# Gate data in a PSUM bank, a ramp on four banks and re-ordered queues in a gated cross-attention and LoRA-expert kernel

## The chip, the core and the metric

The kernel runs on one core of one Trainium2 chip. The metric is the device time in microseconds (us) of one execution; smaller is better.

## What is computed

x is 2x1024x2048 in float32, the context 2x2048x2048. The kernel computes, cut to what matters:

```python
def fake_quant(x, s, z): return (clip(round(x / s + z), 0, 255) - z) * s
# layer 1
q1, q2 = fake_quant(layernorm(x)), fake_quant(ctx)
x = x + tanh(g_xattn) * matmul(q1, q2)              # per batch 1024x2048 by 2048x2048
# layer 2
n = layernorm(x)
logits = n @ route_w.T                              # 8 experts
v, e = top_k(logits, 1)                             # one expert for each row
h = n @ A.T                                         # 8 experts x rank 16 = 128 columns
wh = one_hot(e) * v * h
x = x + tanh(g_ffn) * (wh @ Bw.T)
```

## The kernel before, in words

The 2048 rows of x are 16 tiles t of 128 rows; tiles 0 to 7 belong to batch 0, tiles 8 to 15 to batch 1. A *unit* (t, nb) is one tile by 512 of the 2048 output columns, 16 matmuls of 128x128 by 512, issued in four runs of four: `main(t, nb, run)`. The context of a batch comes in 16 *pieces* of 1 MB, four for each nb; each is loaded, scaled to int8 on ACT (`affine_ctx`) and widened to bf16 into `q2` on POOL or ACT (`widen_ctx`). Batch 1 overwrites the same `q2` behind the last use by tile 7.

A tile goes through these steps, and each engine has its own list of calls, written out by hand in a fixed order; an engine that waits holds everything behind it in its list:

- `load_x(t)` on the SP queue, `stats1(t)` on DVE, `first_norm(t)` on POOL, `affine_x(t)` on ACT (int8 into `x8`), `widen_x(t)` (bf16 into `q1`; DVE for tiles 0 to 3, POOL behind). Then q1 is transposed: for tiles 0 to 5 by TensorE into the two `turn` banks (`turn_q1`) and copied out by DVE (`take_q1T`), for the others by a DMA transpose on the SP queue (`flip_q1`).
- `main` on PE; `add_main(t, nb)` on DVE adds the unit to x and takes its statistics (lines 963 to 970); `stats2_sum` closes them.
- `second_norm(t)` on POOL, then for tiles 3 to 14 `norm_high` and `norm_full` on ACT, `low_rows(t)` on POOL (line 533, a 128x2048 subtraction in SBUF), and two DMA transposes `flip_high` and `flip_low`. For tiles 0, 1, 2 and 15 the transposes go through PE (`turn_y`), ACT (`high_part`) and DVE (`low_part`); for tile 15 the norm itself is done in four groups on DVE (`norm_group`).
- `h_rows_high`, `h_rows_low` (or `h_group`) on PE give h and the logits in the PSUM bank `hp`. `gate(t)` on DVE (lines 982 to 1011), a chain of 13 instructions on 128x136 or 128x128 elements and smaller, picks the expert and scales: `hl` (line 985), the maximum and its index, `pick` (993), `wh` (996), its absolute maximum, and the two halves `whs` (1007, 1009). `hl`, `pick` and `wh` are tiles in SBUF. `turn_wh` on PE (line 1459), `take_wh` on ACT, `expert_product` on PE into the two `outp` banks (1470 to 1472) and `add_experts` on DVE (1015), then `store(t)`.

PSUM has eight banks: two `mainp`, two `turn`, `hp`, `wp`, two `outp`. The unit n uses `mainp[n % 2]`, so unit n waits for the `add_main` of unit n-2. The first four tiles are worked column block by column block (`RAMP`, the *ramp*), because the context arrives only as fast as it is loaded. x tiles share eight places (`HOME`), so `load_x(t)` for t above 5 mostly waits for the store of an earlier tile. A and the router are scaled by DVE in place (`scale_a`, `scale_router`, lines 1022 and 1027).

Of the kernel before, what the change touches and what calls it, by code (L numbers as in the profile page):

```python
# [33 lines left out]
QD = 6  # L34
YD = 3
YP = {0: 0, 1: 1, 2: 2, T - 1: YD}
# [12 lines left out]

XD = 4  # L50


def build(nc, x, ctx, g_x, g_f, x1_scale, x1_zp, x2_scale, x2_zp, route_w, A, Bw, out):
# [13 lines left out]
    with st:  # L67
# [16 lines left out]
        s_half_stored = sem("half_stored")  # L84
# [54 lines left out]
        s_affine1 = sem("affine1")  # L139
        s_q1_ready = sem("q1_ready")  # L140
# [15 lines left out]
        s_y_ready = sem("y_ready")  # L156
        s_y_turned = sem("y_turned")
# [9 lines left out]
        s_h_read = sem("h_read")  # L167
# [3 lines left out]
        s_pick_done = sem("pick_done")  # L171
# [11 lines left out]
        s_outp_read = sem("outp_read")  # L183

# [20 lines left out]
        hl = sb("hl", [P, WC], f32)  # L205
# [4 lines left out]
        pick = sb("pick", [P, ER], f32)  # L210
        wh = sb("wh", [P, ER], f32)
# [4 lines left out]
        eid_i = wh[:, :].bitcast(i32)  # L216
# [7 lines left out]
        diag = pick  # L224
# [45 lines left out]
        ynq = yn[:, :, :].rearrange("p a n -> p (a n)").bitcast(bf16)  # L270
        early = [yT[:, :, :, :].rearrange("p a k m -> p (a k m)").bitcast(f32), y[:, :], stage[:, 0, :], stage[:, 1, :]]
# [34 lines left out]

        def turn_free(kind, t, b):

            if kind == "q":
                return s_q1T_dve, 2 * t + b + 1  # L310
# [4 lines left out]
            return s_y_split, 4 * YP[t] + 3 + b  # L315

# [3 lines left out]
        def _(sp):  # L320
# [35 lines left out]
            def store(t):  # L356
                sp.wait_ge(s_outp_read, NB * (t + 1))
                sp.dma_start(out_t[t], xcol(t, 0, D)).then_inc(s_stored[t % 4], 16)

            def flip_q1(t):  # L360

                sp.wait_ge(s_main_done, UNIT[t - 2, NB - 1] + 1)
# [27 lines left out]
            load_x(4)  # L390
# [3 lines left out]
            load_ctx(12)  # L394
            load_ctx(13)
# [31 lines left out]
            load_ctx(28)  # L427
            store(4)
            load_ctx(29)
            load_x(9)  # L430
            flip_high(6)
            flip_low(6)
            flip_q1(8)
            load_ctx(30)
            load_ctx(31)
            store(5)
            flip_high(7)
# [3 lines left out]
            load_x(11)  # L441
            flip_high(8)
# [3 lines left out]
            load_x(12)  # L446
            load_x(13)
            flip_high(9)
            flip_low(9)
            flip_q1(11)  # L450
            store(7)
            load_x(14)
            flip_high(10)
            flip_low(10)
            flip_q1(12)
            flip_high(11)
            store(8)
            flip_low(11)
            load_x(15)
            flip_q1(13)  # L460
# [4 lines left out]
            flip_high(13)  # L465
            flip_low(13)
# [3 lines left out]
            store(10)  # L470
# [4 lines left out]
            for half in range(2):  # L475
                sp.wait_ge(s_outp_read, NB * (T - 1) + 2 * (half + 1))
                sp.dma_start(out_t[T - 1][:, half * D // 2:(half + 1) * D // 2],
                             xcol(T - 1, half * D // 2, (half + 1) * D // 2)).then_inc(s_half_stored, 16)
            for n in range(4):
                sp.wait_ge(s_stored[n], 16 * len([t for t in range(T - 1) if t % 4 == n]))  # L480
            sp.wait_ge(s_half_stored, 32)
# [1450 lines left out]
```

## Time and profile before

| | us |
|---|---|
| median of 3 runs (389.13 to 390.45) | 389.33 |
| profiled execution, its time | 389.91 |
| profiled execution, its span | 388.10 |
| TensorE busy | 338.8 |
| VectorE busy | 292.3 |
| ScalarE busy | 186.1 |
| GpSimd busy | 166.4 |

The span is what the trace covers; the time lies 1.81 us above it. Starts are counted from the start of the span. PE is TensorE, PEld its weight loads, DVE VectorE, ACT ScalarE, POOL GpSimd, SPq the queue that issues the DMAs. L12 is line 12 of the kernel before. In a row of the timeline the square bracket gives the idle time of the engine in front of the instruction and what ended it.

### The profile page before, as it was taken

Reading aid. Unit: us, or ns where it says so; the run is one execution under the profiler, and the core shown is the slowest. Engines: PE = TensorE matmul, PEld = TensorE weight load, DVE = VectorE, ACT = ScalarE, POOL = GpSimd, SP = SyncE. Lnnn points to the kernel's source line nnn. Section 1 sums busy time; section 2 is a strip of 40 time slices with the busy share of each in tenths; the row PEclk is TensorE's granted clock in tenths of the full one; section 3 lists DMA queues with packets and bytes.
Section 4 is the critical chain, followed back from the end, with each engine's and each line's share of the span. In section 5 each row is a group of like instructions: output and inputs, shape, how many; then the busy total and the mean of one; then the engine's idle time right before and its main releaser. Section 6 shows DMA issues by size and latency. Waiting matters only on the chain.

```text
span 388.1 us, 5794 instructions
## 1 busy us (share of the span) xinstructions
PE 338.8 (87%) x2204; PEld 186.8 (48%) x2230; DVE 292.3 (75%) x578; ACT 186.1 (48%) x119; POOL 166.4 (43%) x219
## 2 busy tenths in 40 slices
PE   0169899999999879998596999999999899998883
PEld 0145344657667536435162364645464546464461
DVE  3989975787988888875688576798764566758785
ACT  1697574868668414488289442422640602440020
POOL 2766566232113740389449226183635162524000
PEclk9999999999999999999699899999999999999999
DMA  7999999096557995999989943976849961277625
GB/s 304 407 366 386 395 387 353 22 389 207 177 194 277 185 233 199 353 246 320 190 131 331 252 150 69 315 160 192 213 85 249 230 118 20 54 119 169 258 110 216
DMA packets 93618, 87.63 MB, mean 226 GB/s; under 512 B 71812, under 2 KB 72836, under 8 KB 89476
## 3 DMA queue, kind: packets, MB, share of 16 engines
q1 hardware_dynamic: 93568, 87.11, 76.4%
q8 instruction: 26, 0.43, 0.4%
q14 instruction: 12, 0.10, 0.1%
q10 hardware_dynamic: 12, 0.00, 0.0%
HBM read 52.49 MB, written 16.78 MB: 178 GB/s over the span
## 4 chain that ended last, share of the span: by engine, by line
PE 64%; DVE 19%; DMA 10%; issue 3%; ACT 2%; POOL 1%; ACTq 0%; DVEq 0%
PE main L1407 44%; DMA qa<-q 6%; PE hp L1428 3%; PE hp L1432 3%; PE hp L1429 3%; PE outp L1470 3%; PE outp L1472 2%; PE outp L1471 2%; DVE whs L1007 2%; DVE pick L993 2%; DVE bn L839 2%; DMA xs<-in_x 2%; DVE xs L1015 1%; DMA prow<-in_g_ffn 1%; DVE wh L996 1%
## 5 line engine op out<-in xcount | busy, mean ns | idle before, releaser
L1407 PE MATMUL main<-q,qa 128*128 128x512 bf16 x875 | 204.7, 387 | 6.8 <-DMA qa<-q 2.4
L1407 PEld LDWEIGHTS main<-q,qa 128*128 128x128 bf16 x896 | 87.8, 99 | 110.2 <-issue 7.2
L533 POOL TENSOR_TENSOR yn<-y,yn 128x2048 f16<-128x2048 f32 x12 | 48.9, 4075 | 32.9 <-ACT y L694 32.7
L967 DVE SCALAR_TENSOR_TENSOR xs<-main,cc,xs 128x512 f32<-128x512 f32 x52 | 38.6, 743 | 29.8 <-PE main L1407 29.6
L540 POOL CAST q<-c 128x2048 bf16<-128x2048 int8 x24 | 45.2, 1905 | 24.9 <-ACT c L650 17.1
L650 ACT ACTIVATE c<-stage,zpc,inv 128x2048 int8<-128x2048 f32 x24 | 49.6, 2086 | 11.2 <-DMA stage<-in_ctx 11.1
L518 POOL TENSOR_SCALAR ve<-mv 128x1 f32<-128x1 f32 x16 | 3.5, 220 | 90.8 <-DVE mv L974 90.8
L1015 DVE SCALAR_TENSOR_TENSOR xs<-outp,tsc,xs 128x512 f32<-128x512 f32 x52 | 36.8, 734 | 6.0 <-PE outp L1472 5.8
L688 ACT ACTIVATE yn<-xs,sc 128x2048 f16<-128x2048 f32 x10 | 20.9, 2092 | 42.5 <-POOL sc L527 42.5
L662 ACT ACTIVATE x<-xs,sc 128x2048 int8<-128x2048 f32 x13 | 27.2, 2090 | 27.6 <-POOL sc L513 25.1
L839 DVE BATCH_NORM_STATS2 bn<-xs 128x6 f32<-128x512 f32 x52 | 32.0, 676 | 7.8 <-DMA xs<-in_x 7.8
L970 DVE BATCH_NORM_STATS2 bn<-xs 128x6 f32<-128x512 f32 x52 | 36.1, 694 | 1.8
L1428 PE MATMUL hp<-WT,yT 128*128 128x136 f16 x256 | 35.8, 223 | 0.3 <-DVE yT L979 0.3
L1429 PE MATMUL hp<-WT,yT 128*128 128x136 f16 x256 | 35.8, 223 | 0.0
L699 ACT ACTIVATE whT<-wp 128x256 f16<-128x256 f16 x16 | 6.0, 378 | 61.2 <-PE wp L1459 61.2
L1470 PE MATMUL outp<-BT,whT 128*128 128x512 f16 x64 | 24.4, 380 | 5.6 <-DVE xs L1015 3.7
L550 POOL CAST q<-x 128x2048 bf16<-128x2048 int8 x12 | 22.7, 1893 | 14.9 <-ACT x L662 14.4
L1407 PE MATMUL main<-q,yn 128*128 128x512 bf16 x123 | 28.5, 379 | 0.3
L1428 PEld LDWEIGHTS hp<-WT,yT 128*128 128x128 f16 x256 | 25.0, 98 | 2.5 <-DVE yT L979 0.4
L1429 PEld LDWEIGHTS hp<-WT,yT 128*128 128x128 f16 x256 | 25.1, 98 | 2.0
L1432 PE MATMUL hp<-WT,yT 128*128 128x136 f16 x256 | 25.1, 223 | 0.0
L1471 PE MATMUL outp<-BT,whT 128*128 128x512 f16 x64 | 24.3, 379 | 0.0
(122 smaller groups left out, 423.6 us busy)
## 6 DMA issues: line engine op xcount, KB each, us to landing
stage<-in_ctx SPq DMA_DIRECT2D x24, 1024.0 KB, 7.6
xs<-in_x SPq DMA_DIRECT2D x13, 1024.0 KB, 6.7
out<-xs SPq DMA_DIRECT2D x12, 1024.0 KB, 5.7
yT<-in_ctx SPq DMA_DIRECT2D x4, 1024.0 KB, 10.6
y<-in_ctx SPq DMA_DIRECT2D x4, 1024.0 KB, 10.6
c<-in_x SPq DMA_DIRECT2D x3, 1024.0 KB, 7.1
out<-c SPq DMA_DIRECT2D x3, 1024.0 KB, 6.3
c<-in_L_ffn_A SPq DMA_DIRECT2D x1, 1024.0 KB, 15.9
```

The costliest lines, as they stand in the source:

```text
L533: pool.tensor_tensor(yn[:, 1, :], y[:, :], yn[:, 0, :], ALU.subtract).then_inc(s_ylo_made, 1)
L540: pool.tensor_copy(in_q2(piece), c8_of(piece)).then_inc(s_ctx_ready, 1)
L650: act.activation(c8_of(piece), place(piece), ACT.Identity, bias=zpc[:, 1:2], scale=inv[:, 1:2])\
L839: dve.bn_stats(bn1[:, t % 2, nb, :], xcol(t, nb * NW, (nb + 1) * NW)).then_inc(s_bn1_done, 1)
L967: dve.scalar_tensor_tensor(out=xcol(t, c0, c1), in0=mainp[n % 2][:, :], scalar=cc[:, :], in1=xcol(t, c0, c1), op0=ALU.mult, op1=ALU.add).t ...
L970: dve.bn_stats(bn2[:, t % G, nb, :], xcol(t, c0, c1)).then_inc(s_bn2_done, 1)
L1015: dve.scalar_tensor_tensor(out=xcol(t, g * NW, (g + 1) * NW), in0=outp[g % 2][:, :], scalar=tsc[:, t:t + 1], in1=xcol(t, g * NW, (g + 1) * ...
L1407: last = pe.matmul(mainp[n % 2][:, :], q1T(t)[:, k, :], q2[:, nb, k, :], start=(k == 0), stop=(k == KC - 1))
L1428: pe.matmul(hp[:, 0:WC], yT[:, 0, c, :], WT[:, c, 0:WC], start=(c == 0), stop=False)
L1429: pe.matmul(hp[:, 0:WC], yT[:, 0, c, :], WT[:, c, WC:2 * WC], start=False, stop=False)
L1432: return pe.matmul(hp[:, 0:WC], yT[:, 1, c, :], WT[:, c, 0:WC], start=False, stop=(c == KC - 1))
L1470: pe.matmul(o, whT[:, 0, :], BT[:, 0, g * NW:(g + 1) * NW], start=True, stop=False)
```

## The change

- **Gate.** `hl` and `wh` become column ranges of the PSUM bank `hp` (columns 144 to 279 and 288 to 415, behind h's 0 to 135). `pick` and its instruction go: one `scalar_tensor_tensor` writes `wh` = (index equal) * hl, and the factor top8, which pick carried, goes into `tsc`. The gate has 12 instructions. The next tile's h, which overwrites the bank, now waits for `s_wh_ready` (the gate's end) where it waited for `s_h_read` (its first instruction).
- **First tile.** `affine_x(0)` and `widen_x(0)` are split in two halves of 1024 columns, `turn_q1(t, half)` and `take_q1T(t, half)` are separate calls, and `main(t, 0, run)` waits for the half of q1T that it reads.
- **Four banks.** Units 0 to 11 rotate over `mainp` and `outp`; `spread_scales`, which uses `outp[0]`, waits for the `add_main` of unit 11.
- **ACT.** It scales A and the router (`mult_a`, `mult_router`) in place of DVE, and takes the last group of tile 15's norm.
- **Orders.** All five lists are re-ordered. The last store goes out in four parts in place of two. Among the moves on the SP queue: `load_x(4)` goes behind four more pieces, `load_ctx(25)` and `load_ctx(26)` ahead of `load_x(6)` and `load_x(7)`, `load_x(9)` behind `flip_q1(8)`, `flip_high(6)` ahead of `store(4)`, `flip_q1(13)` ahead of `load_x(15)`. On PE the two units in work are interleaved run by run in many tiles; `turn_q1(2)` goes behind the first run of `main`.

```diff
+N4 = 12
...
-        hl = sb("hl", [P, WC], f32)
...
-        pick = sb("pick", [P, ER], f32)
-        wh = sb("wh", [P, ER], f32)
...
         hp = bank("hp")
+        hl, wh = hp[:, 144:144 + WC], hp[:, 288:288 + ER]
...
+        ramp_banks = mainp + outp
...
+        def bank_of(n):
+            return ramp_banks[n % 4] if n < N4 else mainp[n % 2]
...
             def gate(t):
+
                 n = t + 1
                 dve.wait_ge(s_h_done, n)
-                dve.tensor_tensor(hl[:, :], hp[:, 0:WC], wscale[:, :], ALU.mult).then_inc(s_h_read, 1)
-                dve.wait_ge(s_h_read, n)
+                dve.tensor_tensor(hl, hp[:, 0:WC], wscale[:, :], ALU.mult).then_inc(s_hl_done, 1)
+                dve.wait_ge(s_hl_done, n)
...
-                dve.tensor_scalar(pick[:, :], eid[:, :], idxf[:, :], top8[:, 0:1], ALU.is_equal, ALU.mult)\
-                   .then_inc(s_pick_done, 1)
-                dve.wait_ge(s_pick_done, n)
-                dve.tensor_tensor(wh[:, :], hl[:, 0:ER], pick[:, :], ALU.mult).then_inc(s_wh_done, 1)
+                dve.scalar_tensor_tensor(out=wh, in0=eid[:, :], scalar=idxf[:, :], in1=hl[:, 0:ER],
+                                         op0=ALU.is_equal, op1=ALU.mult).then_inc(s_wh_done, 1)
...
-                dve.tensor_scalar(tsc[:, t:t + 1], am[:, 1:2], th[:, 1:2], None, ALU.mult).then_inc(s_tsc_done, 1)
+                dve.tensor_scalar(tsc[:, t:t + 1], am[:, 1:2], th[:, 1:2], top8[:, 0:1], ALU.mult, ALU.mult)\
+                   .then_inc(s_tsc_done, 1)
...
-                dve.tensor_scalar(whs[:, 0, :], wh[:, :], am[:, 2:3], None, ALU.mult).then_inc(s_wh_high, 1)
+                dve.tensor_scalar(whs[:, 0, :], wh, am[:, 2:3], None, ALU.mult).then_inc(s_wh_high, 1)
...
             def h_rows_high(t):
-                pe.wait_ge(s_h_read, t)
-                pe.wait_ge(s_yhiT_loaded, 16 * (t - YD + 1))
+                pe.wait_ge(s_wh_ready, t)
+                pe.wait_ge(s_yhiT_loaded, 16 * (YN.index(t) + 1))
...
+            def affine_first(half):
+                c0, c1 = half * D // 2, (half + 1) * D // 2
+                act.wait_ge(s_norm1, 1)
+                act.activation(x8[:, c0:c1], xcol(0, c0, c1), ACT.Identity, bias=sc1[:, 0, 2:3], scale=sc1[:, 0, 1:2])\
+                   .then_inc(s_affine1 if half else s_affine_half, 1)
...
+            def mult_a():
+                act.wait_ge(s_consts, 4)
+                act.wait_ge(s_wmax_step, 3)
+                act.activation(a_nat, a_nat, ACT.Identity, bias=zero[:, :], scale=wmax[:, 2:3]).then_inc(s_a_scaled, 1)
...
-            turn_q1(0)
-            turn_q1(1)
-            turn_q1(2)
+            turn_q1(0, 0)
+            turn_q1(0, 1)
+            turn_q1(1, 0)
+            turn_q1(1, 1)
             column_sums(0, [0])
             main(0, 0, 0)
+            turn_q1(2, 0)
+            turn_q1(2, 1)
             main(0, 0, 1)
-            turn_q1(3)
```

## Rows read from the trace of the kernel before

**Rows 1.** The page: busy time, share of the span and instructions.
```profile
PE 338.8 (87%) x2204; PEld 186.8 (48%) x2230; DVE 292.3 (75%) x578; ACT 186.1 (48%) x119; POOL 166.4 (43%) x219
```

**Rows 2.** Waits of PE: line, what ended them, us in total, times, longest.
```profile
PE wp L1459 <- DVE whs L1009: 11.0, 3, 5.5
...
PE outp L1470 <- DVE xs L1015: 3.7, 3, 2.3
PE main L1407 <- DMA qa<-q: 2.4, 3, 1.3
...
PE main L1407 <- DVE xs L967: 1.4, 2, 1.1
...
PE outp L1470 <- DVE c L1015: 0.9, 1, 0.9
```

**Rows 3.** Stretches: length, busy by engine (instructions), PE clock, DMA share, GB/s.
```profile
125.00:155.00 30.00, 26.57 (x201) 15.14 (x201) 25.27 (x62) 10.68 (x7) 12.86 (x13) 1.00 0.85 210
155.00:187.00 32.00, 27.33 (x161) 13.69 (x161) 23.12 (x41) 23.84 (x13) 23.48 (x28) 1.00 1.02 304
187.00:220.00 33.00, 27.02 (x142) 12.96 (x144) 24.41 (x36) 21.82 (x14) 17.85 (x17) 0.84 1.01 212
```

**Rows 4.** Gate instructions by line: duration in ns, min/median/max.
```profile
L993 DVE TENSOR_SCALAR pick<-eid,idxf,top x16: 345/346/3601, 98.4 to 377.8; 128x128 f32<-128x128 f32 x16
L996 DVE TENSOR_TENSOR wh<-hl,pick x16: 291/292/1866, 98.8 to 378.1; 128x128 f32<-128x128 f32 x16
L1007 DVE TENSOR_SCALAR whs<-wh,am x16: 285/286/4105, 99.8 to 379.2; 128x128 f16<-128x128 f32 x16
```

**Rows 5.** Timeline around tile 5's gate, POOL, then DVE (start, us).
```profile
178.96 4.08 POOL L533 TENSOR_TENSOR yn<-y,yn 128x2048 f16<-128x2048 f32 x1
182.98 5.63 POOL L540 CAST q<-c 128x2048 bf16<-128x2048 int8 x3
...
180.92 2.20 DVE L993 TENSOR_SCALAR pick<-eid,idxf,top 128x128 f32<-128x128 f32 x1
183.16 1.86 DVE L996 TENSOR_TENSOR wh<-hl,pick 128x128 f32<-128x128 f32 x1
...
186.88 1.86 DVE L1009 SCALAR_TENSOR_TENSOR whs<-wh,am,whs 128x128 f16<-128x128 f32 x1
```

**Rows 6.** Timeline of PE: both long stalls and the matmuls behind them.
```profile
188.81 0.40 PE L1459 MATMUL wp<-idh,whs 128*128 128x128 f16 x2 [5.47 <-DVE whs L1009]
189.47 9.59 PE L1407 MATMUL main<-q,qa 128*128 128x512 bf16 x32 [0.27 <-DVE xs L967]
...
214.21 0.29 PE L1459 MATMUL wp<-idh,whs 128*128 128x128 f16 x2 [3.69 <-DVE whs L1009]
...
216.61 7.34 PE L1407 MATMUL main<-q,qa 128*128 128x512 bf16 x29 [0.22 <-issue]
...
347.19 7.07 PE L1407 MATMUL main<-q,qa 128*128 128x512 bf16 x32
```

**Rows 7.** Timeline of the ramp: PE, and POOL's widening of piece 7.
```profile
24.94 1.86 PE L1337 MATMUL turn<-idb,q 128*128 128x128 bf16 x16 [3.35 <-DVE qa L884]
26.60 3.62 PE L1407 MATMUL main<-q,qa 128*128 128x512 bf16 x8
...
46.89 4.26 PE L1407 MATMUL main<-q,qa 128*128 128x512 bf16 x19
...
41.84 2.01 POOL L540 CAST q<-c 128x2048 bf16<-128x2048 int8 x1 [0.81 <-ACT c L650]
```

**Rows 8.** Timeline of the SP queue: one DMA transpose of q1.
```profile
297.36 5.55 SPq L364 DMA_TRANSPOSE qa<-q x1
```

**Rows 9.** Timeline of DVE in the tail, then the last stores.
```profile
368.86 1.00 DVE L1060 TENSOR_SCALAR y<-xs,sc 128x512 f32<-128x512 f32 x2
...
376.75 0.30 DVE L985 TENSOR_TENSOR hl<-hp,wscale 128x136 f32<-128x136 f32 x1 [0.43 <-PE hp L1432]
...
383.19 1.41 DVE L1015 SCALAR_TENSOR_TENSOR xs<-outp,tsc,xs 128x512 f32<-128x512 f32 x2 [0.26 <-PE outp L1472]
```

More of the change, by code:

```diff
@@ L441, in _ @@
             load_x(11)
+            load_x(12)
             flip_high(8)
@@ L455, in _ @@
             flip_q1(12)
+            store(7)
+            store(8)
+            load_x(14)
             flip_high(11)
-            store(8)
             flip_low(11)
+            flip_q1(13)
             load_x(15)
-            flip_q1(13)
             store(9)
@@ L783, in _ @@
             widen_ctx(18)
+            affine_ctx(28)
+            take_wh(5)
             widen_ctx(19)
@@ L827, in _ @@
             high_part(15, 0)
-            take_wh(14)
             high_part(15, 1)
+            norm_group(15, 3)
             high_part(15, 2)
             high_part(15, 3)
+            take_wh(14)
             take_wh(15)
@@ L1026, in scale_router, with mult_a, mult_router @@
                 scale_of(rmax, r_nat, s_rmax_step)
+            def mult_a():
+                dve.tensor_scalar(a_nat, a_nat, wmax[:, 2:3], None, ALU.mult).then_inc(s_a_scaled, 1)
+            def mult_router():
                 dve.tensor_scalar(r_nat, r_nat, rmax[:, 2:3], None, ALU.mult).then_inc(s_r_scaled, 1)
@@ L1139, in _ @@
             low_part(1, 3)
-            stats1(5)
+            add_main(4, 1)
+            gate(1)
             add_experts(0, 0)
-            gate(1)
             add_experts(0, 1)
@@ L1276, in _ @@
             add_main(14, 2)
-            add_experts(11, 3)
+            add_experts(11, 0)
+            add_experts(11, 1)
             add_main(14, 3)
             stats2_sum(14)
+            add_experts(11, 2)
+            gate(13)
+            tile_terms(15)
+            add_main(15, 0)
+            add_experts(11, 3)
             add_experts(12, 0)
@@ L1282, in _ @@
             add_experts(12, 2)
-            gate(13)
-            tile_terms(15)
-            add_main(15, 0)
             add_main(15, 1)
@@ L1329, in wait_turn, with turn_q1 @@
                     pe.wait_ge(s, count)
-            def turn_q1(t):
-                pe.wait_ge(s_q1_ready, t + 1)
-                for half in range(2):
-                    wait_turn("q", t, half)
-                    for k in range(KC // 2):
-                        c = half * KC // 2 + k
-                        last = pe.transpose(turnb[half][:, k * P:(k + 1) * P], q1[:, c * P:(c + 1) * P], idb[:, :])
-                    last.then_inc(s_q1T_turned, 1)
+            def turn_q1(t, half):
+                if t == 0 and half == 0:
+                    pe.wait_ge(s_q1_half, 1)
+                elif t == 0 or half == 0:
+                    pe.wait_ge(s_q1_ready, t + 1)
+                wait_turn("q", t, half)
+                for k in range(KC // 2):
+                    c = half * KC // 2 + k
+                    last = pe.transpose(turnb[half][:, k * P:(k + 1) * P], q1[:, c * P:(c + 1) * P], idb[:, :])
+                last.then_inc(s_q1T_turned, 1)
             def turn_a(c):
@@ L1556, in _ @@
             main(1, 3, 2)
+            main(1, 3, 3)
             spread_scales()
-            turn_q1(4)
-            main(1, 3, 3)
             column_sums(2, [3])
@@ L1875, in _ @@
             main(15, 1, 1)
+            main(15, 2, 0)
             main(15, 1, 2)
             main(15, 1, 3)
-            main(15, 2, 0)
+            expert_product(12, 1)
             main(15, 2, 1)
+            expert_product(12, 2)
+            expert_product(12, 3)
+            turn_wh(13)
             h_rows_high(14)
```

689 lines of the change are left out of this document (383 added, 306 removed).

## The prediction

> **What bounds the kernel now.** I read the page first: TensorE is busy 338.8 of 388.1 us, the next engine, DVE, 292.3 [rows 1]. So PE is the bound, and a change is worth what it takes from PE's 49.3 idle us or from matmul time at the low clock. The waits of PE say where the idle time behind the ramp lies: turn_wh (line 1459) waits for the end of the gate three times, 11.0 us; expert products wait for add_experts, 3.7 and 0.9 us; main waits for a DMA transpose 2.4 us and for add_main 1.4 us [rows 2]. Next the stretches: 155 to 187 and 187 to 220 hold 4.7 and 6.0 us of idle PE, and the second runs at a mean clock of 0.84 [rows 3]. Last the gate's own instructions. Three of them have a median of 0.29 to 0.35 us and a longest of 1.87 to 4.11 us [rows 4]. In tile 5's gate pick takes 2.20, wh 1.86 and the second whs 1.86 us, while POOL runs a 4.08 us subtraction in SBUF and then three casts one after the other; pick ends at 183.12, where POOL goes from the one to the other, and the next long ones end with casts [rows 5]. I read this as a shared resource: a gate instruction that needs it waits for POOL's instruction to end.
>
> The Trainium skill, page "SBUF — State Buffer", section "Who interferes with whom", has the rule: VectorE and GpSimd share one pair of SBUF ports as an exclusive lock, and a VectorE instruction takes it in a two-port mode or with two SBUF inputs. The rows fit (a tensor_scalar, a tensor_tensor and a scalar_tensor_tensor with two SBUF inputs are the long ones), and by it the new gate is free, since every instruction over 128 columns has hl or wh in PSUM as an input and at most one input in SBUF.
>
> **Gate.** It runs 16 times. pick goes (0.35 us each), and the waits for POOL go. What that is worth is read on PE. Tile 5: stall of 5.47, then 0.27 waiting for add_main, which stood behind the gate; then 32 matmuls in 9.59 us, where 32 elsewhere take 7.07: 2.5 us, at 1.2 in place of 2.4 GHz for part of it, after PE had stood still [rows 6]. Tile 6: 3.69, then 0.22; then the 36 matmuls to the next expert product last from 214.50 to 223.95, 9.45 us less the 0.22, where 36 at full clock take 36/32 x 7.07 = 7.95: 1.3 us [rows 6]. Tile 4: pick took up to 3.60 us [rows 4], and an expert product then waited 2.3 for add_experts [rows 2]. Tile 13: the first whs took 4.11 [rows 4], and main then waited 1.1 for add_main [rows 2]. Sum: 5.47 + 0.27 + 2.5 + 3.69 + 0.22 + 1.3 + 2.3 + 1.1 = **16.9 us**, all on the path. The third wait of line 1459, 11.0 - 5.47 - 3.69 = 1.8 us, is the last tile's gate and belongs to the tail.
>
> Whether an instruction that reads and writes PSUM costs more: hl, which reads PSUM, takes 0.30 us for 136 columns [rows 9], wh from SBUF 0.29 for 128 [rows 4]. I take no difference; 0.1 us an instruction would be 0.6 us a gate, hidden for all tiles but the last.
>
> The skill speaks against the change here: "VectorE: DVE Perf Modes", section "The TRN2 errata", gives a VectorE instruction with a PSUM source a fixed part of 120 cycles where an SBUF source has 58. The two rows above don't show it at this size. By the page's figures, an estimate, about 62 cycles at 0.96 GHz on five or so instructions would add 0.3 us to each gate and to the end of the kernel.
>
> The added wait: h of tile t+1 may start only when gate t is done, some 2.4 us later than before. Behind it on PE stands the whole rest of the list. In the new list turn_wh(t), which waits for the same event anyway, stands ahead of h(t+1) for most tiles; where it doesn't (h of tiles 1, 3, 13 and 15), at least 16 matmuls of main lie between, 3.5 us at 7.07 for 32 [rows 6]. Taken at nothing; rival 3 prices it where this cover is gone.
>
> **Ramp.** Before, the first main starts at 26.60 because turn_q1(2) stands ahead of it and waits 3.35 us for DVE [rows 7]. After, main(0,0,0) needs only the first half of tile 0's q1T and piece 0, both ready by then, and stands behind turn_q1(1); I put it at about 24.2. A fixed end bounds the gain: main(0,1,3), the fourth run that needs piece 7, starts at 46.89, and piece 7 is widened at 41.84 + 2.01 = 43.85; its load runs with the DMA queues full. So at most 3.0 us can come out at that point, 4.0 if the piece lands 1 us earlier (its buffer comes free before affine_x(3) now). The four banks and the two scalings moved to ACT serve to reach it: they take the add_main wait of the ramp away. At the other end is 0, if DVE, which has the same casts and copies to do, sets the pace. I take **2.5 us**, near the upper bound, because the waits of PE behind the ramp are all priced below and none of them is for a piece [rows 2]. mult_a and mult_router (an estimate of 2 us each, four times the 0.50 us of 512 columns in norm_group [rows 9]) lie in ACT's waits for pieces; without that cover they delay a piece by up to 4 us, and that too is the 0 end.
>
> **Flips and loads.** Of the 2.4 us of waits for a transposed q1 and the 0.9 for an expert product, the new SP order removes what stands behind `load_x(15)`: that transpose took 5.55 us to issue alone [rows 8], and it now goes first. The others depend on x loads, which wait for stores. I take **1.5 us**; between 0 and 3.3.
>
> **Tail.** From norm_group(15,0) at 368.86 to the last gate's start at 376.75 are 7.9 us [rows 9]. DVE has in between four groups, four expert adds and four low parts. The new order leaves it three groups, three adds (two of them behind the last low part) and four low parts: 0.5 us less for the group, 0.7 for the add; pick takes 0.35 off the last gate, and the last store is a quarter of a tile in place of a half, perhaps 0.5 us sooner down. But two expert adds of tile 14 go behind the gate, 1.4 us more on DVE after it. Terms that are independent of each other: +1.2 +0.4 +0.5, and of the two adds about half hidden under turn_wh, take_wh and the first product: -0.7. **1.4 us**, between 0 and 2.
>
> **What comes late next.** Without the stalls PE reaches main(8) about 14 us sooner after main(7) and the pieces of batch 1, x(8), x(9) and the flips must be there. The DMA queues are full for the whole of 155 to 220, share 1.02 and 1.01 [rows 3]. The new order moves two loads ahead of it and x(9) behind the flips; 125 to 155 has 0.15 x 30 = 4.5 us of free queue. New small stalls are likely: x(6) is now behind piece 25, one more megabyte, up to 2.6 us at gate(2) by my walk through the lists. I add back **3.0 us**, between 0 and 10.
>
> **The sum.** 16.9 + 2.5 + 1.5 + 1.4 - 3.0 = 19.3 us. Against the profiled execution: 389.9 - 19.3 = 370.6; the median lies 0.6 below that execution, so **370.0 us**.
>
> **Rivals.**
> 1. *The DMA queues become the bound of 155 to 220.* For it: both shares at 1.0 [rows 3], and 14 of the 16.9 us lie there. Then of these 14 only the 4.5 us of free queue before can be won, 9.5 come back in place of my 3.0: 370.0 + 6.5 = 376.5. Against it: part of the share is transposes, which nobody waited for more than 1.3 us [rows 2], and the loads stand in a better order. Chance 0.22.
> 2. *The gate still waits for POOL.* If the lock isn't a matter of SBUF inputs, wh and both whs can still be held; only pick's share goes (3.60 - 0.35 and 2.20 - 0.35 us in tiles 4 and 5 [rows 4, 5]). The stalls of tiles 5, 6 and 13 then stay for the most part, some 11 of the 16.9: 381. Against it: hl, with one input in PSUM, stands in the same gates and was never long, and neither were the adds from PSUM. 0.07.
> 3. *The bank that h and the gate share stops PE.* If h(t+1) stands right behind h(t), it waits the gate out: 2.4 us x 15 = 36 us, less the 19.3: 389.3 + 16.7 = 406. It decides from where PE comes to h(t+1) less than 2.7 us after h(t); eight tiles of it cancel the gain. Against it: a tile's 64 matmuls of main, 14 us, lie between them for most tiles. 0.04, with 0.02 for a smaller form that ends within 0.3%.
>
> **Chances and range.** Forecast 0.65 (364 to 373), rivals 0.22, 0.07 and 0.06. The measurement can tell 0.3%, 1.2 us, from no change. Faster by more 0.94, within 0.02, slower 0.04. The low end takes all upper bounds without the add-back: 389.3 - 16.9 - 4.0 - 3.3 - 2.0 = 363.1; the high end takes rival 1 with the lower bounds of the ramp: 379. Range 364 to 379.
>
> **What the profile after would show.** Gate: no instruction of it above 0.4 us, line 993's kind gone, DVE busy at most 292 less the 12 us that the five long ones of rows 4 and 5 lose, 5.5 for pick and 4 for the scalings, 271 us, no wait on turn_wh over 1 us but in the tail. Clock 1.00 between 187 and 220. Ramp: first main near 24, the run main(0,1,3) near 44. Rival 1: main waiting for flips or widened pieces between 150 and 205. Rival 2: long whs or wh with POOL busy beside them. Rival 3: h waiting for whs. Wrong would be the prediction if PE's idle time between 50 and 350 came out above 8 us.

## The result and the profile after

The changed kernel takes 371.79 us (median of 4 runs, 370.97 to 372.98). The kernel before, run beside it on the same chip, takes 389.89 (389.13 to 390.77). The ratio is 0.9537, with a 95% interval of 0.9498 to 0.9577. The profiled execution took 371.14 us with a span of 369.4, against 389.9 and 388.1 before: 18.7 us are gone from the span. The forecast was 19.3 us for the profiled execution and 370.0 for the median.

First the page of the kernel after, busy time by engine, to be laid beside [rows 1]:

```profile
PE 334.0 (90%) x2230; PEld 185.6 (50%) x2230; DVE 266.6 (72%) x560; ACT 190.9 (52%) x123; POOL 166.0 (45%) x219
```

PE has the same matmuls to do (the smaller count in [rows 1] is one of records) and spends 4.8 us less on them; the rest of the gain is idle time. DVE lost 25.7 us of busy time, of which pick (5.5) and the two scalings (4) are 9.5 by the prediction's estimate. Most of the rest is time that gate instructions had spent held up: the four kinds of lines 993, 996, 1007 and 1009, whose tiles all lay in SBUF, took 38.8 us before, 18.4 more than 16 times their medians. The forecast was at most 271 us of busy DVE; it is 266.6.

The waits of PE in the kernel after (line, what ended them, us in total, times, longest), beside [rows 2]:

```profile
PE outp L1442 <- DMA prow<-in_g_ffn: 8.4, 1, 8.4
PE turn L1462 <- DVE qa L990: 6.1, 1, 6.1
PE turn L1462 <- DVE q L981: 5.7, 1, 5.7
PE turn L1554 <- DVE y L1177: 2.6, 1, 2.6
PE main L1534 <- DMA qa<-q: 2.0, 2, 1.3
PE outp L1601 <- DVE xs L1127: 1.8, 2, 1.6
PE main L1534 <- POOL q L584: 1.6, 2, 0.9
PE outp L1601 <- ACT whT L763: 1.0, 2, 0.5
PE main L1534 <- DVE xs L1073: 0.9, 1, 0.9
PE outp L1601 <- DVE c L1127: 0.4, 1, 0.4
```

The top line of [rows 2], 11.0 us of turn_wh waiting for the gate, has no successor here. The first three lines are the start of the kernel. Line 1554 and the 1.6 of line 1601 are the tail.

The three stretches of [rows 3], after (length, busy by engine with instructions, PE clock, DMA share, GB/s):

```profile
125.00:155.00 30.00, 29.60 (x213) 16.53 (x211) 23.58 (x61) 14.45 (x9) 10.88 (x18) 1.00 0.97 252
155.00:187.00 32.00, 29.73 (x173) 14.59 (x172) 20.45 (x41) 22.91 (x15) 23.95 (x24) 1.00 1.02 263
187.00:220.00 33.00, 32.24 (x222) 17.65 (x220) 24.14 (x55) 23.04 (x13) 19.99 (x27) 1.00 1.01 287
```

PE's idle time falls from 3.4, 4.7 and 6.0 us to 0.4, 2.3 and 0.8, and the clock of the last stretch from 0.84 of full speed is back at 1.00. The DMA share of the last two was already 1.0 and stays there. Between 50 and 350, the stretch for which the prediction had named 8 us of idle PE as the sign of being wrong, PE is idle for 6.0 us (16.4 before).

The gate's instructions over 128 columns besides hl and the reduction, by line (ns, min/median/max), the answer to [rows 4]. The data of hl and wh now lie in the tile hp:

```profile
L1106 DVE SCALAR_TENSOR_TENSOR hp<-eid,idxf,hp x16: 356/356/356, 100.4 to 356.6; 128x128 f32<-128x128 f32 x16
L1119 DVE TENSOR_SCALAR whs<-hp,am x16: 341/342/343, 101.5 to 357.8; 128x128 f16<-128x128 f32 x16
L1121 DVE SCALAR_TENSOR_TENSOR whs<-hp,am,whs x16: 350/351/352, 101.9 to 358.2; 128x128 f16<-128x128 f32 x16
```

Minimum and maximum of each line are now within 2 ns of each other, where the maxima were 1.87 to 4.11 us.

Timeline of the kernel after, PE, then POOL's widening of piece 7 (start, us; idle time before in brackets), beside [rows 6, 7]:

```profile
24.23 1.91 PE L1534 MATMUL main<-q,qa 128*128 128x512 bf16 x4
...
43.91 1.03 PE L1534 MATMUL outp<-q,qa 128*128 128x512 bf16 x4
...
158.61 3.63 PE L1534 MATMUL main<-q,qa 128*128 128x512 bf16 x16 [0.90 <-DVE xs L1073]
...
169.60 3.63 PE L1534 MATMUL main<-q,qa 128*128 128x512 bf16 x16 [1.28 <-DMA qa<-q]
...
211.69 7.08 PE L1534 MATMUL main<-q,qa 128*128 128x512 bf16 x32 [0.76 <-DMA qa<-q]
...
340.93 4.48 PE L1534 MATMUL main<-q,qa 128*128 128x512 bf16 x20
...
349.26 1.11 PE L1554 MATMUL turn<-idf,y 128*128 128x128 f32 x8 [2.55 <-DVE y L1177]
...
41.56 1.89 POOL L584 CAST q<-c 128x2048 bf16<-128x2048 int8 x1 [1.23 <-ACT c L705]
```

The rows cut the span in three parts at main(0,1,3) and at the end of the last run of main. The latter ends at 340.93 + 4.48 = 345.41 in the kernel after. In the kernel before it is this row, which ends at 365.44:

```profile
361.82 3.62 PE L1407 MATMUL main<-q,qa 128*128 128x512 bf16 x16
```

| part of the span | before, us | after, us | difference | forecast |
|---|---|---|---|---|
| start to main(0,1,3) | 46.89 | 43.91 | -3.0 | -2.5 |
| from there to the end of main | 318.55 | 301.50 | -17.0 | -16.9 - 1.5 + 3.0 = -15.4 |
| end of main to the end | 22.66 | 23.99 | **+1.3** | **-1.4** |
| span | 388.1 | 369.4 | -18.7 | -19.3 |

The tail moved against the forecast. DVE of the kernel after in its last 21 us, the answer to [rows 9], and then the SP queue of the stores (start and length of the issue):

```profile
348.65 1.00 DVE L1177 TENSOR_SCALAR y<-xs,sc 128x512 f32<-128x512 f32 x2
...
355.62 0.31 DVE L1098 TENSOR_TENSOR hp<-hp,wscale 128x136 f32<-128x136 f32 x1 [0.20 <-PE hp L1562]
...
358.44 1.40 DVE L1127 SCALAR_TENSOR_TENSOR xs<-outp,tsc,xs 128x512 f32<-128x512 f32 x2
360.10 1.41 DVE L1127 SCALAR_TENSOR_TENSOR xs<-outp,tsc,xs 128x512 f32<-128x512 f32 x2 [0.26 <-PE outp L1603]
362.17 1.41 DVE L1127 SCALAR_TENSOR_TENSOR xs<-outp,tsc,xs 128x512 f32<-128x512 f32 x2 [0.66 <-PE outp L1603]
363.83 1.41 DVE L1127 SCALAR_TENSOR_TENSOR xs<-outp,tsc,xs 128x512 f32<-128x512 f32 x2 [0.26 <-PE outp L1603]
...
355.44 6.42 SPq L402 DMA_DIRECT2D out<-xs  x2
362.94 2.79 SPq L521 DMA_DIRECT2D out<-xs  x4
```

The SP queue of the kernel before in its tail:

```profile
371.21 10.31 SPq L358 DMA_DIRECT2D out<-xs  x2
382.96 2.00 SPq L477 DMA_DIRECT2D out<-xs  x2
```

From norm_group(15,0) to the start of the last gate are now 7.0 us (7.9 before), 0.9 of the 1.2 us that the sum had. Behind the gate stand eight adds in place of six. The first SP row of each fence holds store(13) and store(14). store(14) is out at 355.44 + 6.42 = 361.86, that is 6.2 us after the gate's start; before it was 371.21 + 10.31 = 381.52, 4.8 us after 376.75. From there to the end of the span are 7.5 us, before 6.6. So the tail reads -1.1 (end of main to the gate) + 1.5 + 0.9 = +1.3.

### The profile page after: what moved, and what is told of

Read it like the earlier page. It is cut to its first block, busy times and chain, and to the rows that moved or that the text cites. A ratio compares the mean times of both kernels' runs of the same rounds, so it can differ in the third digit from the quotient of the medians.

```text
span 369.4 us, 5825 instructions
## 1 busy us (share of the span) xinstructions
PE 334.0 (90%) x2230; PEld 185.6 (50%) x2230; DVE 266.6 (72%) x560; ACT 190.9 (52%) x123; POOL 166.0 (45%) x219
## 4 chain that ended last, share of the span: by engine, by line
PE 65%; DMA 11%; POOL 9%; DVE 6%; ACT 3%; issue 2%; SPq 1%; ACTq 0%; POOLq 0%; DVEq 0%
PE main L1534 40%; PE outp L1534 6%; POOL q L584 4%; DMA xs<-in_x 4%; DMA qa<-q 3%; PE hp L1558 3%; PE hp L1559 3%; PE hp L1562 3%; DMA out<-xs 3%; PE outp L1601 2%; POOL yn L577 2%; PE outp L1603 2%; PE outp L1602 2%; DMA prow<-in_g_ffn 2%; PE turn L1554 2%
## 5 line engine op out<-in xcount | busy, mean ns | idle before, releaser
L1534 PE MATMUL main<-q,qa 128*128 128x512 bf16 x880 | 199.5, 380 | 4.6 <-DMA qa<-q 2.0
L1534 PEld LDWEIGHTS main<-q,qa 128*128 128x128 bf16 x880 | 85.0, 98 | 104.7 <-DMA qa<-q 3.0
L705 ACT ACTIVATE c<-stage,zpc,inv 128x2048 int8<-128x2048 f32 x24 | 49.8, 2087 | 11.3 <-DMA stage<-in_ctx 11.3
L584 POOL CAST q<-c 128x2048 bf16<-128x2048 int8 x24 | 46.1, 1937 | 17.7 <-ACT c L705 16.8
L1073 DVE SCALAR_TENSOR_TENSOR xs<-main,cc,xs 128x512 f32<-128x512 f32 x46 | 34.1, 741 | 21.2 <-PE main L1534 20.7
L1127 DVE SCALAR_TENSOR_TENSOR xs<-outp,tsc,xs 128x512 f32<-128x512 f32 x52 | 36.9, 739 | 14.2 <-PE outp L1603 14.1
L723 ACT ACTIVATE x<-xs,sc 128x2048 int8<-128x2048 f32 x12 | 25.0, 2087 | 17.1 <-POOL sc L557 12.1
L592 POOL CAST q<-x 128x2048 bf16<-128x2048 int8 x12 | 22.7, 1891 | 24.1 <-ACT x L723 18.0
L1601 PE MATMUL outp<-BT,whT 128*128 128x512 f16 x64 | 24.3, 380 | 3.2 <-DVE xs L1127 1.8
L1602 PE MATMUL outp<-BT,whT 128*128 128x512 f16 x64 | 24.3, 379 | 0.0
L1603 PE MATMUL outp<-BT,whT 128*128 128x512 f16 x64 | 24.3, 379 | 0.0
```

The costliest lines, as they stand in the source:

```text
L584: pool.tensor_copy(in_q2(piece), c8_of(piece)).then_inc(s_ctx_ready, 1)
L705: act.activation(c8_of(piece), place(piece), ACT.Identity, bias=zpc[:, 1:2], scale=inv[:, 1:2])\
L1073: dve.scalar_tensor_tensor(out=xcol(t, c0, c1), in0=bank_of(n)[:, :], scalar=cc[:, :], in1=xcol(t, c0, c1), op0=ALU.mult, op1=ALU.add).the ...
L1127: dve.scalar_tensor_tensor(out=xcol(t, g * NW, (g + 1) * NW), in0=outp[g % 2][:, :], scalar=tsc[:, t:t + 1], in1=xcol(t, g * NW, (g + 1) * ...
L1534: last = pe.matmul(bank_of(n)[:, :], q1T(t)[:, k, :], q2[:, nb, k, :], start=(k == 0), stop=(k == KC - 1))
L1601: pe.matmul(o, whT[:, 0, :], BT[:, 0, g * NW:(g + 1) * NW], start=True, stop=False)
```

## The experiments

The theory under test: most of the gain comes from the place of the gate's data, since a gate instruction is held up by POOL only where all its tiles lie in SBUF. Its rivals are the wait of h, the new orders of the queues, and the ramp. Ratios are to the kernel before run beside each, with 95% intervals. The experiments ran on several chips, so two versions are compared by the difference of their ratios, times 389.9; the difference of the medians stands beside it where the two disagree.

**gate_only.** The kernel before with the gate of the kernel after, and the wait that it needs. Ramp, orders and stores stay. Two helpers that had borrowed the room of wh and pick get tiles of their own, as in the kernel after.

```diff
-        hl = sb("hl", [P, WC], f32)
...
-        pick = sb("pick", [P, ER], f32)
-        wh = sb("wh", [P, ER], f32)
...
+        hl, wh = hp[:, 144:144 + WC], hp[:, 288:288 + ER]
...
-                dve.tensor_scalar(pick[:, :], eid[:, :], idxf[:, :], top8[:, 0:1], ALU.is_equal, ALU.mult)\
-                   .then_inc(s_pick_done, 1)
-                dve.wait_ge(s_pick_done, n)
-                dve.tensor_tensor(wh[:, :], hl[:, 0:ER], pick[:, :], ALU.mult).then_inc(s_wh_done, 1)
+                dve.scalar_tensor_tensor(out=wh, in0=eid[:, :], scalar=idxf[:, :], in1=hl[:, 0:ER],
+                                         op0=ALU.is_equal, op1=ALU.mult).then_inc(s_wh_done, 1)
...
-                    pe.wait_ge(s_h_read, t)
+                    pe.wait_ge(s_wh_ready, t)
```

> The kernel before with the gate of the change alone (hl and wh in the PSUM bank of h, pick folded into wh, h waiting for the gate's end); every list in its old order. Theory (the shared resource cost 16.9 us): the two long waits for whs (5.47 and 3.69 us) and the low clock between 187 and 220 go, no gate instruction lasts over 0.4 us; up to 16.9 us less, and what is late next in the old order takes 2 to 4 of it back: 373 to 377 us against 389.9. Rival (the new orders made the gain, the gate only fits into them): 383 us or more.

Measured: 376.20 us, ratio 0.9640 (0.9590 to 0.9689), span 373.7. One row of PE's timeline of this kernel, the longest wait behind the ramp:

```profile
191.04 0.22 PE L1424 MATMUL hp<-WT,yT 128*128 128x136 f16 x1 [3.09 <-DMA yT<-yn]
```

No gate instruction lasts over 0.36 us. The gate alone is worth 0.036 x 389.9 = 14.0 us (12.1 to 16.0 by the interval). The row is what then comes late: h(6) waits for its transposed tile, which stands in the old SP order behind a store and an x load. Its last main ends at 351.28, so 14.2 us are won up to there and 0.3 in the tail (22.4 us for 22.7).

**gate_pick_sbuf.** The same with hl and wh in PSUM, but pick kept as it was, a tensor_scalar from SBUF to SBUF (shown against gate_only; the factor top8 goes back from `tsc` into pick):

```diff
-                dve.scalar_tensor_tensor(out=wh, in0=eid[:, :], scalar=idxf[:, :], in1=hl[:, 0:ER],
-                                         op0=ALU.is_equal, op1=ALU.mult).then_inc(s_wh_done, 1)
+                dve.tensor_scalar(pick[:, :], eid[:, :], idxf[:, :], top8[:, 0:1], ALU.is_equal, ALU.mult)\
+                   .then_inc(s_pick_done, 1)
+                dve.wait_ge(s_pick_done, n)
+                dve.tensor_tensor(wh, hl[:, 0:ER], pick[:, :], ALU.mult).then_inc(s_wh_done, 1)
```

> As gate_only, but pick stays: an instruction with one SBUF input and an SBUF output. Theory (an instruction is held by POOL when it reads SBUF alone into SBUF, or reads two SBUF inputs): pick stays long in the gates of tiles 4 to 6 (up to 3.6 us), wh and both whs stay at 0.3 to 0.4 us; the time lies between gate_only and before, 376 to 383 us. Rival (anything that touches the bank or the timing of h is what freed the gate): no long pick, same time as gate_only plus 16 x 0.35 us of DVE at most.

Measured: 381.16 us, ratio 0.9749 (0.9710 to 0.9788). Two of its gate instructions by line, as above:

```profile
L992 DVE TENSOR_SCALAR pick<-eid,idxf,top x16: 344/347/4123, 98.1 to 367.1; 128x128 f32<-128x128 f32 x16
L1006 DVE TENSOR_SCALAR whs<-hp,am x16: 349/351/353, 99.5 to 368.6; 128x128 f16<-128x128 f32 x16
```

In one kernel two instructions of one kind: the one between SBUF tiles is held up to 4.1 us, the one that reads PSUM never. The longest pick starts at 136.40, 0.04 us behind a 4.07 us subtraction of POOL. Of PE's waits, turn_wh has 4.3 us (1.7 in gate_only) and the expert products wait 4.2 us for add_experts (1.4). Against gate_only only pick and its factor differ, and that costs 0.0109 x 389.9 = 4.2 us. So the place of the operands is the cause of the long instructions. Not every kind is held in SBUF: the reduction read `wh` there before and never took over 0.289 us, in tile 5's gate at 185.05 too, in the middle of POOL's casts [rows 5].

**wait_only.** The kernel before, with the new wait of h alone.

```diff
-                    pe.wait_ge(s_h_read, t)
+                    pe.wait_ge(s_wh_ready, t)
```

> The kernel before with one edit: h of the next tile waits for the gate's end (s_wh_ready) and not for its first instruction. Theory (taken at nothing): within 0.5 us of before, 389 to 391 us, no wait of h for whs over 0.5 us in total. Rival (the held bank costs PE): up to 2.4 us a tile, over 393 us.

Measured: 389.93 us, ratio 0.9985 (0.9960 to 1.0010), span 387.6. No wait on an h appears that was not there before. The cover holds in the old lists; the kernel after, with the new ones, shows no wait on h either, and rival 3 falls.

**after_gate_sbuf.** The kernel after, hl and wh moved back to SBUF. The fused instruction, all orders and the ramp stay.

```diff
-        hl, wh = hp[:, 144:144 + WC], hp[:, 288:288 + ER]
+        hl_t, wh_t = sb("hl", [P, WC], f32), sb("wh", [P, ER], f32)
+        hl, wh = hl_t[:, :], wh_t[:, :]
```

> The kernel after the change with hl and wh as tiles in SBUF again, all else (orders, folded pick, four banks) as changed. Theory: wh (two SBUF inputs) and both whs are held by POOL again where they overlap its subtractions and casts, single instructions of 1.8 to 4 us return, and 6 to 15 us come back: 378 to 387 us. Rival (the orders keep gates and POOL apart by themselves): 372 us, no long instruction.

Measured: 389.56 us, ratio 0.9967 (0.9939 to 0.9994), span 390.1. Its timeline around one gate (POOL, DVE, PE), and then its PE clock in two stretches:

```profile
182.12 4.07 POOL L578 TENSOR_TENSOR yn<-y,yn 128x2048 f16<-128x2048 f32 x1
182.23 4.11 DVE L1107 SCALAR_TENSOR_TENSOR wh<-eid,idxf,hl 128x128 f32<-128x128 f32 x1
186.13 5.68 POOL L585 CAST q<-c 128x2048 bf16<-128x2048 int8 x3
188.20 1.86 DVE L1122 SCALAR_TENSOR_TENSOR whs<-wh,am,whs 128x128 f16<-128x128 f32 x1
190.12 0.40 PE L1590 MATMUL wp<-idh,whs 128*128 128x128 f16 x2 [5.47 <-DVE whs L1122]
190.78 9.24 PE L1535 MATMUL main<-q,qa 128*128 128x512 bf16 x32 [0.27 <-DVE xs L1074]
```
```profile
125.00:155.00 30.00, 26.79 (x180) 14.41 (x181) 22.54 (x47) 10.79 (x7) 9.62 (x15) 0.89 0.73 179
187.00:220.00 33.00, 27.64 (x172) 14.50 (x174) 23.93 (x40) 22.46 (x13) 20.10 (x19) 0.90 0.62 180
```

The fused instruction begins 0.11 us after POOL's subtraction and ends with it (186.34 and 186.19). PE stands still for the same 5.47 us as in [rows 6], and the 32 matmuls behind it take 9.24. The answer is clear and the size was missed: nearly the whole gain is gone, (0.9967 - 0.9537) x 389.9 = 16.8 us (17.8 by the medians), where 6 to 15 were expected. In the new order other gates meet POOL (add_main is waited for 5.8 us in total, in four places, where [rows 2] has 1.4). So all the other parts of the change together are worth (0.9640 - 0.9537) x 389.9 = 4.0 us once the gate is free (4.4 by the medians), and 0.33% of 389.9, 1.3 us, while it is not. The two figures differ by less than their intervals allow for, so that these parts are worth more once the gate is free is suggested, not shown.

**two_banks.** The kernel after without the four banks of the ramp.

```diff
-N4 = 12
+N4 = 0
```

> The kernel after the change with N4 = 0: the ramp's units use two banks again. Theory: the ramp's 3.0 us need the four banks in part, because DVE falls behind with copies and scalings; PE waits for add_main again between 35 and 44, main(0,1,3) starts 0.5 to 2 us later than 43.9, and so does the end: 372.5 to 374 us. Rival (the order alone does it): within 0.3 us of the changed kernel.

Measured: 373.49 us, ratio 0.9546 (0.9503 to 0.9589), span 371.9. main(0,1,3) starts at 44.30, 0.4 us later, and add_main is waited for three times, 1.5 us, in place of once, 0.9. The median lies 1.7 above that of the kernel after, the ratio only 0.0009, 0.4 us, and the intervals overlap, so a gain of the banks beyond the 0.4 us at the ramp isn't shown.

**first_whole.** The kernel after with tile 0 scaled and widened in one piece.

```diff
-            affine_first(0)
-            affine_first(1)
+            affine_x(0)
...
-            widen_first(0)
-            widen_first(1)
+            widen_x(0)
```

> The kernel after the change with the first tile scaled and widened whole. Theory: turn_q1(0) starts 0.4 us later, but turn_q1(1) waits for DVE's copy behind stats1(3) until 22.5 in any case, and piece 7 comes at 43.9: no change of the time, within 0.3 us. Rival (the halves carry part of the ramp's gain): 0.5 to 1.3 us slower.

Measured: 371.75 us, ratio 0.9504 (0.9454 to 0.9554), span 369.7, main(0,1,3) at 43.68. The halves do nothing that shows.

**scale_dve.** The kernel after with mult_a and mult_router back on DVE.

```diff
             affine_ctx(4)
-            mult_a()
...
             scale_a()
+            mult_a()
...
             affine_ctx(10)
-            mult_router()
...
             scale_router()
+            mult_router()
```

> The kernel after the change with A and the router scaled by DVE again, directly behind their maxima. Theory: 2.3 and 1.6 us more in DVE's list at 31 and 36; four banks cover part; main(0,1,3) 0 to 2 us later, 372 to 374 us. Rival (ACT's cover was not free: pieces come sooner without it): 0.5 us faster.

Measured: 372.29 us, ratio 0.9527 (0.9483 to 0.9572), span 369.9. main(0,1,3) moves to 45.00, 1.1 us later, and the median doesn't follow; no difference is shown.

**x9_early.** The kernel after, with the SP order of before around flip_high(6).

```diff
-            flip_high(6)
             store(4)
+            load_x(9)
+            flip_high(6)
             flip_low(6)
             flip_q1(8)
-            load_x(9)
```

> The kernel after the change with three SP steps in the old order: store(4), load_x(9), and only then flip_high(6), flip_low(6), flip_q1(8). Theory (the queue order around tile 8 is what keeps the full DMA queues from becoming the bound): flip_high(6) waits for the store's landing, 6 to 8 us later than 176.1, main(8) or h(6) waits 1 to 4 us, 373 to 376 us. Rival (the queues have slack there): within 0.5 us.

Measured: 375.13 us, ratio 0.9583 (0.9529 to 0.9636), span 373.4. The SP queue in this kernel, PE behind it, and then the SP queue of the kernel after:

```profile
181.97 0.33 SPq L374 DMA_DIRECT2D xs<-in_x  x1
182.40 5.00 SPq L413 DMA_TRANSPOSE yT<-yn  x1
...
189.60 0.22 PE L1558 MATMUL hp<-WT,yT 128*128 128x136 f16 x1 [2.28 <-DMA yT<-yn]
```
```profile
176.09 1.86 SPq L413 DMA_TRANSPOSE yT<-yn  x1
178.00 1.07 SPq L402 DMA_DIRECT2D out<-xs  x1
```

The transpose goes out 6.3 us later, takes 5.00 us to issue in place of 1.86, and PE waits for it, as h(6) did in gate_only. The last main ends at 348.22, 2.8 us later. By the traces this one order carries the greater part of the 4.0 us of the other parts. By the ratios it is 0.0046, 1.8 us, by the medians 3.3, and the intervals overlap: its size stays open, though each of its four times (373.24 to 375.99) lies above each of the kernel after (370.97 to 372.98).

**old_tail.** The kernel after, with the lists of DVE, PE and ACT before and around gate(15) in the order of before (and all four LN2 groups on DVE).

```diff
-LAST_ACT = [3]
+LAST_ACT = []
...
-            gate(15)
             add_experts(14, 0)
...
             add_experts(14, 1)
+            gate(15)
             add_experts(14, 2)
             add_experts(14, 3)
```

> The kernel after the change with the lists of PE, DVE and ACT from expert_product(13,2) on as before the change (all four norm groups on DVE, two of tile 14's adds ahead of the last gate). From the end of main(15) to the end of the span the kernel before takes 22.7 us and the changed one 24.0. Theory (eight adds behind the last gate in place of six cost more than the shorter way to the gate gives): 1 to 1.7 us faster than the changed kernel. Rival (the last stores are what is late): no faster.

Measured: 370.21 us, ratio 0.9498 (0.9476 to 0.9520), span 368.0. Its SP queue:

```profile
350.44 10.12 SPq L402 DMA_DIRECT2D out<-xs  x2
361.34 3.07 SPq L521 DMA_DIRECT2D out<-xs  x4
```

Its gate starts later (355.98, 11.3 us after its last main, where the kernel after has 10.2), yet store(14) is out at 360.56, 1.3 us sooner than in the kernel after, and the tail is 23.3 us for 24.0. The median is 1.6 us lower, the ratio 0.0039, and the two intervals overlap by 0.2%: a gain is likely, by span and median alike, but not shown beyond doubt.

**halves.** The kernel after, with the last store in two parts as before.

```diff
-            for g in range(NB):
-                sp.wait_ge(s_outp_read, NB * (len(OUT_DVE) - 1) + g + 1)
...
+            for half in range(2):
+                sp.wait_ge(s_outp_read, NB * (len(OUT_DVE) - 1) + 2 * (half + 1))
...
```

> The kernel after the change with the last store in two parts. In the changed kernel the last add ends at 365.24 and the span at 369.40, 4.2 us; before it was 384.6 and 388.1, 3.5 us. Theory (the quarters queue behind store(14), which now goes out 3.5 us before the last add, and gain nothing): within 0.4 us of the changed kernel. Rival (the four parts cost issue time): 0.4 to 0.7 us faster.

Measured: 371.24 us, ratio 0.9530 (0.9506 to 0.9553), span 368.9. From the end of store(14)'s issue, 356.10 + 6.26 = 362.36, to the end are 6.5 us, where the kernel after has 7.5. But its store(14) comes 0.5 us later, behind a stretch at low clock. The same window of its trace and of the kernel after's (columns as in [rows 3]):

```profile
349.00:352.00 3.00, 3.00 (x12) 1.68 (x11) 2.19 (x4) 1.90 (x3) 0.00 (x0) 0.53 0.03 5
```
```profile
349.00:352.00 3.00, 2.74 (x18) 1.81 (x18) 2.97 (x6) 1.78 (x3) 0.00 (x0) 1.00 0.02 5
```

In both PE had stood still for 2.6 us, until 348.29 in halves and until 349.26 in the kernel after. In the one PE then runs at about 1.2 GHz and gets 12 matmuls done, in the other at 2.4 GHz and 18. In the median nothing is shown: 0.6 us, with overlapping intervals.

**act_pool_tail.** The kernel after, with the expert part of tile 14 scaled by ACT and added by POOL, so that DVE has no add of tile 14 left.

```diff
-OUT_ACT = []
+OUT_ACT = [14]
...
-            add_experts(14, 0)
-            add_experts(14, 1)
-            add_experts(14, 2)
-            add_experts(14, 3)
...
+            add_part(14, 0)
+            add_part(14, 1)
+            add_part(14, 2)
+            add_part(14, 3)
```

> The kernel after the change with tile 14's expert adds off DVE: ACT scales each product out of PSUM (0.6 us), POOL adds it to x (1.0 us by a quarter of its 4.08 us subtraction). Theory (DVE's adds behind the last gate and store(14) behind them are what is late): store(14) goes out 1 us sooner and the four adds behind the gate are tile 15's alone; 2 us faster than the changed kernel, 369 to 370 us. Rival (POOL's adds hold DVE or come late, or the last stores' bytes are the bound): no faster than 0.5 us.

Measured: 373.41 us, ratio 0.9576 (0.9549 to 0.9604), span 371.6: slower than the kernel after, if anything. Its rows of POOL and SP:

```profile
358.87 4.94 POOL L604 TENSOR_TENSOR xs<-xs,yn 128x512 f32<-128x512 f32 x4 [11.30 <-ACT yn L814]
...
356.45 7.71 SPq L402 DMA_DIRECT2D out<-xs  x2
```

One add on POOL takes 1.26 us, where DVE's takes 0.74, and store(14) is out at 364.16 in place of 361.86. The theory that any relief of DVE behind the gate helps falls in this form: the tile is waited for, not the engine. Part of the 2.2 us that its span is longer is a low clock here too (0.50 between 349 and 352); how much isn't told apart.

**old_tail_halves.** Both edits together: the old order of the tail and two parts of the last store.

```diff
-LAST_ACT = [3]
+LAST_ACT = []
...
-            gate(15)
             add_experts(14, 0)
...
             add_experts(14, 1)
+            gate(15)
...
-            for g in range(NB):
...
+            for half in range(2):
...
```

> old_tail with the last store in two parts. From the end of the issue of store(14) to the end of the span lie 7.5 us in the changed kernel, 7.4 in old_tail, 7.4 in act_pool_tail, all with four parts, and 6.5 with two parts (halves) and 6.6 before. Theory (the last two stores, 2 MB, are late as a whole, and four parts cost them 0.9 us): 0.6 to 0.9 us faster than old_tail, 369.3 to 369.6 us, span 367.1. Rival (the last add plus a fixed landing is the end): the same as old_tail.

Measured: 369.78 us (369.05 to 370.65), ratio 0.9489 (0.9460 to 0.9518), span 368.2. It is the fastest version of the study, 2.0 us or 0.5% below the median of the kernel after. Its interval overlaps that of the kernel after by 0.2%, and it can't be told from old_tail (370.21), where 0.6 to 0.9 us less were expected. In its profiled execution the last expert products of tile 15 fell on a low clock; its window, and old_tail's:

```profile
361.00:363.00 2.00, 2.00 (x6) 0.59 (x5) 1.16 (x2) 0.00 (x0) 0.00 (x0) 0.50 0.95 393
```
```profile
361.00:363.00 2.00, 1.65 (x7) 0.42 (x6) 1.74 (x4) 0.00 (x0) 0.00 (x0) 1.00 1.03 422
```

So its last add ends at 365.03, 1.4 us after old_tail's (363.64). From the end of store(14)'s issue, 360.65, to the end of the span are then 7.5 us although the last store has two parts, and 3.2 from the last add.

## Why the prediction was right, and where it was not

**What bounds the kernel** was read rightly: PE, with its idle time between 155 and 220 and the low clock behind it.

**Gate, 16.9 us.** Right in mechanism and nearly in size. gate_only won 14.0 with the old orders, and the loss of the gate's place in the new kernel cost 16.8 by the ratios; the term of 16.9 stands at the upper end. What was counted is PE's standstill plus the slow matmuls behind it, and not the time of the gate's own instructions; that was the right measure. The Trainium skill's rule on who holds the SBUF ports ("SBUF — State Buffer", "Who interferes with whom"), by which the new gate is free, is borne out by gate_pick_sbuf: the one SBUF-to-SBUF tensor_scalar reaches 4123 ns, the PSUM one 353.

**No difference for operands in PSUM.** Nearly. By the medians hl, which read PSUM before too and now also writes it, took 0.307 us (0.299 before), wh 0.356 (0.352 in SBUF in after_gate_sbuf), the reduction 0.291 (0.286), the second whs 0.351 (0.350). One did change: the first whs, a tensor_scalar, took 0.342 in place of 0.286. The Trainium skill's page "VectorE: DVE Perf Modes" ("The TRN2 errata") spoke against the change with 62 cycles more for each instruction, an estimated 0.065 us. The first whs shows 0.056 and the others 0.00 to 0.01, so the trace doesn't agree for most of them. `tsc`, which now takes a second scalar operand, went from 0.194 to 0.255.

**Added wait, nothing.** Right, shown by wait_only for the old lists and by the waits of the kernel after for the new ones.

**Ramp, 2.5 us.** 3.0 by the rows, the upper bound named. The first main starts at 24.23 (forecast 24.2) and main(0,1,3) at 43.91, 0.46 after the widening of piece 7 ends at 43.45. Of its means, the halves brought nothing, the banks 0.4 us at that point and the scalings 1.1. No one of them shows in the median; they were priced only together, and together is all that can be said for certain.

**Flips and loads 1.5, late next -3.0.** Their sum with the gate came out at 17.0 for 15.4. The transpose behind `load_x(15)`, for which PE had waited 1.33 us at 306.53, is waited for no more, and the expert product's wait fell from 0.9 to 0.4: 1.8 us in place of 1.5. Late next was less than the 3.0 taken: 0.9 for an add_main at 158.61, 0.76 for a transpose at 211.69, and 0.4 more for the one at 169.60 (1.28 for 0.90), 2.0 us. That leaves 17.2 for the gate, an estimate from these rows. Rival 1 asked for waits on flips or pieces worth 9.5; there are 2.0. PE's idle time in the two stretches with a DMA share of 1.0 fell from 10.7 to 3.0 us while the share stayed, so the share was no bound of that size; in x9_early and in gate_only the order within the queue cost PE waits of 2.3 and 3.1 us.

**Tail, 1.4 us: this step failed, and its sign was wrong.** It came out at -1.3. The half before the gate was nearly right: 0.9 of gain from norm_group to the gate, where 1.2 was forecast. The gate itself got shorter by 0.2 us (3.09 to 2.90, from the start of hl to the end of the second whs) and not by the 0.4 taken for pick, because the fused instruction, `tsc` and the first whs each take longer. Wrong was the belief that about half of the two adds would hide, and that the quarter store saves 0.5. The kernel ends with 2 MB of stores, and store(14) waits for the adds that were put behind the gate: it is out 1.5 us later against the gate. From the end of store(14)'s issue to the end lie 7.4 to 7.5 us in all eight kernels of this study with the four-part store, act_pool_tail among them, where the last add comes 1.5 us after that issue and not 3.1 to 3.4. With the two-part store they are 6.5 to 6.6 (before, wait_only, gate_only, halves), and 7.5 in gate_pick_sbuf and old_tail_halves, whose last add comes 4.4 us after the issue and is followed by 3.1 and 3.2 us. So the four parts lost 0.9 us in the traces in place of 0.5 won; the medians of halves and old_tail_halves don't show it. The sum of the terms was near by luck in part: ramp and middle came out 2.1 us better than it had them, the tail 2.7 worse.

## What to carry over

Where TensorE waits for a short chain of small VectorE instructions, and GpSimd has instructions of microseconds in SBUF beside it, try the chain's data in free columns of a PSUM bank; it was worth 14.0 to 16.8 us of 390 here. To find such a chain, look for instructions whose longest is many times their median, and price them by the standstill and the slow matmuls that follow on TensorE. When such a stall goes, look at the queue orders around it anew: in gate_only the next wait was one of 3.1 us for a transpose. In a tail, find the stores that the end hangs on, and put ahead whatever they wait for.

## What the runs showed of the hardware

- The clock after a short standstill isn't the same in each execution: after 2.6 us of standing still PE ran at 1.00 in the kernel after, at 0.53 in halves and at 0.50 in act_pool_tail. old_tail and old_tail_halves both stand still for 1.7 us and then for 0.5 before the last expert products; between 361 and 363 the one ran at 1.00, the other at 0.50. What it costs is seen in PE's work: by the window above, 12 matmuls in place of 18 in 3 us. What decides it stays open.
- The gate's tensor_scalar over 128 columns (whs) takes 0.278 and 0.286 us from SBUF (after_gate_sbuf, before) and 0.342 and 0.351 from PSUM (the kernel after, gate_pick_sbuf). The other kinds of the gate over 128 columns differ by 0.00 to 0.01.
- Beside a GpSimd instruction in SBUF, a tensor_scalar, tensor_tensor or scalar_tensor_tensor of the gate with all its tiles in SBUF took up to 4.12, 1.87 and 4.27 us (gate_pick_sbuf, before and after_gate_sbuf). The reduction over an SBUF tile never took over 0.289, and with an operand in PSUM none of the gate took over 0.36 us in the kernel after and gate_only.
- From the end of store(14)'s issue the kernel takes 7.4 to 7.5 us with the last store of 1 MB in four parts (eight kernels) and 6.5 to 6.6 with two (four kernels; 7.5 in the two whose last add is late).
- An fp32 addition on POOL takes 1.26 us for 512 columns (act_pool_tail), where the subtraction of 2048 with a 16-bit result takes 4.08: more than a quarter of it, which would be 1.02.
